# Moving the first normalisation statistics of a long-convolution and expert-mixture kernel beside its scalar setup, and loading its first column set in quarters

## The chip, the cores and the metric

The kernel runs on the 8 cores of one Trainium2 chip. Each core has TensorE (matmuls; PE in the profile), VectorE (DVE), ScalarE (ACT), GpSimd (POOL) and SyncE (SP, which issues DMAs), and 16 DMA engines. The eight cores run the same program on 2,048 of the 16,384 rows each and exchange nothing. The metric is the device time of the slowest core in microseconds.

## The reference

The input `x` has shape (2, 8192, 4096). Two residual layers are applied:

```python
x = x + s4(layernorm(x))
x = x + experts(layernorm(x))

def s4(u):                       # u: rows of length L = 4096
    K = kernel of length L, from Lambda, p, q, Vc, Ct, Bp and log_step
    y = irfft(rfft(u, 2L) * rfft(K, 2L))[..., :L]      # causal convolution
    return y + D[0] * u

def experts(x):                  # 64 experts, 16 of them for each row
    scores = x @ Wr.T            # top 16, softmax: gates G
    h = einsum('nd,krd->nkr', x, A)                    # rank 16
    return einsum('nkr,kdr->nd', h * G[:, :, None], B) * 2
```

The convolution kernel `K` is that of a 64-dimensional complex state-space model. It doesn't depend on `x`, and every core computes what it needs of it.

## The kernel before

All five engines have instruction lists that are written out by hand in program order. Each engine works through its own list in order, and waits on named counters (semaphores) are put between the instructions. `P.wait(eng, name, value)` puts a wait on an engine's list, `P.op(eng, fn, inc=name)` an instruction that raises a counter when it is done, `P.dma` a DMA, which raises its counter by 16 when it has landed and, unless told otherwise, is issued only when all earlier ones of the same counter have landed.

The 2,048 rows of a core are held transposed: 4,096 features in 32 blocks of 128 partitions, and four sets (`s` = 0 to 3) of 512 columns (rows of `x`). A set of float32 is 8 MB. The buffers `U0` and `U1` hold sets in turn.

*Start.* SyncE issues 21 small loads (constants and the state-space parameters, counter `ld0`). GpSimd issues 32 loads of the router weights `wrt_b` with a cast (counter `ldg`). Then all five engines wait for both counters, and SyncE issues set 0 as one DMA of 8 MB (L371, counter `uld`).

*Statistics, `emit_prep1`.* For each of the 32 blocks of a set: ScalarE casts the block to bfloat16 into one of four buffers (L259), TensorE adds it up over the partitions with a matmul into `ps1` (L264), GpSimd squares it (L272), and TensorE adds the squares up into `ps2` (L277). The steps are made in eight groups of four blocks. `emit_chain1` follows with ten instructions, each of which waits for the one before: five on VectorE (L289 to L293), Ln and Exp on ScalarE (L294, L295), one on VectorE (L296), a matmul on TensorE that spreads the result over the partitions (L297), and a copy to `Rb` on ScalarE (L298). For set 0 all of this stands at the start of the program (L372 to L377). For sets 1 to 3 the steps are put between the chunks of the set before.

*Setup of the state-space model, L379 to L565.* Its instructions go through the helper `so`. It makes each wait for all earlier ones, whatever the engine:

```python
def so(eng, fn):
    P.wait(eng, "seq")
    P.wait(eng, "sqd")
    P.wait(eng, "sqg")
    P.op(eng, fn, inc="seq")
```

The first of them is a memset on VectorE (L379), the second an Exp on ScalarE (L382), the next 41 are on VectorE (L383 to the negation ahead of L436), and then come small float32 matmuls in turn with VectorE copies. The setup leaves the convolution's matrices `cm_T`, `cm_ET`, `cm_O1T` and `cm_MtT` (the last one written at L565). Scratch tiles of the setup lie in the memory of `U1`, so SyncE loads set 1 only when the setup is done.

*Correction row.* A short serial chain (L568 to L616) pushes a column of ones through the same convolution, with TensorE (L583 to L604) and ScalarE (`c1stage`, L595, and the state, L607) in turn, and writes `c1row`.

*Main work of the first layer.* For each set, in eight chunks of four blocks: casts (L656), matmuls for the state and the outputs (L676, L699, L705), a product with `Rb` (L715) and the sum with `x` (L720). Each quarter of a set that is done is spilled to DRAM as float32 and bfloat16 (L727, L731). Sets 1 to 3 are loaded in four quarters of 2 MB (L629), one after another. The experts' weights `At_sb` are loaded from GpSimd's queue while set 3 is worked on.

*Second layer.* The spilled sets are read back (`X2`), normalised, scored, multiplied by the experts' first matrices (L965), gated, and multiplied by the second ones (L1053), with the residual sum on VectorE (L1060).

Of the kernel before, what the change touches and what calls it, by code (L numbers as in the profile page):

```python
# [78 lines left out]
def build_nc():  # L79
    nc = bass.Bass("TRN2", target_bir_lowering=False)  # L80

    u_in = nc.dram_tensor("u_in", [NS1, 128, NBLK * F1], F32, kind="ExternalInput")
# [122 lines left out]
    P = Plan(nc)  # L205
# [10 lines left out]
    rb_cnt = {}  # L216
# [7 lines left out]
    UB = [U0, U1]  # L224
# [4 lines left out]
    rb_cnt = {}  # L229
    tcv_after = []  # L230

    def chain(eng, fn):
        P.wait(eng, "sx")
        P.op(eng, fn, inc="sx")

    def uld_full(s):
        return 16 if s == 0 else 16 + 64 * s

    def uld_q(s, b):
        return 16 if s == 0 else 16 + 64 * (s - 1) + 16 * (b // 8 + 1)  # L240

    def emit_prep1(s):
        buf = UB[s % 2]
# [6 lines left out]
        for g8 in range(8):  # L250
            def step(g8=g8):
                for b in range(4 * g8, 4 * g8 + 4):
                    q = b % 2
                    w = b % 4
                    P.wait("scalar", "uld", uld_q(s, b))
                    if b >= 4:
                        P.wait("scalar", "t_s1", base_s1 + (b - 4) + 1)
                        P.wait("scalar", "g_sq", base_gq + (b - 4) + 1)
                    P.op("scalar", lambda e, b=b, w=w: e.copy(  # L259
                        UBF.ap()[:, w * 512:(w + 1) * 512], blk_ap(buf, b)), inc="s_ub")  # L260
                    P.wait("tensor", "s_ub", base_ub + b + 1)
                    if b == 0:
                        P.wait("tensor", "sx", sx_prev)
                    P.op("tensor", lambda e, b=b, w=w: e.matmul(  # L264
                        ps1.ap()[:, :], sumw.ap()[:, :],
                        UBF.ap()[:, w * 512:(w + 1) * 512],
                        start=(b == 0), stop=(b == NBLK - 1),
                        skip_group_check=True), inc="t_s1")
                    P.wait("gpsimd", "s_ub", base_ub + b + 1)
                    if b >= 2:  # L270
                        P.wait("gpsimd", "t_sq", base_sq + (b - 1))
                    P.op("gpsimd", lambda e, b=b, q=q, w=w: e.tensor_mul(  # L272
                        sqs.ap()[:, q * 512:(q + 1) * 512],
                        UBF.ap()[:, w * 512:(w + 1) * 512],
                        UBF.ap()[:, w * 512:(w + 1) * 512]), inc="g_sq")
                    P.wait("tensor", "g_sq", base_gq + b + 1)
                    P.op("tensor", lambda e, b=b, q=q: e.matmul(  # L277
                        ps2.ap()[:, :], sumw.ap()[:, :],
                        sqs.ap()[:, q * 512:(q + 1) * 512],
                        start=(b == 0), stop=(b == NBLK - 1),  # L280
                        skip_group_check=True), inc="t_sq")
# [3 lines left out]
    def emit_chain1(s, base_s1, base_sq):  # L285
        sl = s % 2
        P.wait("vector", "t_s1", base_s1 + NBLK)
        P.wait("vector", "t_sq", base_sq + NBLK)
        chain("vector", lambda e: e.tensor_scalar(M_AP, ps1.ap()[0:1, :], 1.0 / DM, None, ALU.mult))  # L289
        chain("vector", lambda e: e.tensor_scalar(V_AP, ps2.ap()[0:1, :], 1.0 / DM, None, ALU.mult))  # L290
        chain("vector", lambda e: e.tensor_mul(R_AP, M_AP, M_AP))
        chain("vector", lambda e: e.tensor_sub(V_AP, V_AP, R_AP))
        chain("vector", lambda e: e.tensor_scalar(V_AP, V_AP, EPS, None, ALU.add))  # L293
        chain("scalar", lambda e: e.activation(R_AP, V_AP, AF.Ln))  # L294
        chain("scalar", lambda e: e.activation(R_AP, R_AP, AF.Exp, scale=-0.5))  # L295
        chain("vector", lambda e, sl=sl: e.tensor_scalar(negmr.ap()[0:1, sl * 512:(sl + 1) * 512], M_AP, -1.0, None, ALU.mult))  # L296
        chain("tensor", lambda e: e.matmul(psX.ap()[:, :], onesrf.ap()[:, :], R_AP, start=True, stop=True))  # L297
        chain("scalar", lambda e, sl=sl: e.copy(Rb.ap()[:, sl * 512:(sl + 1) * 512], psX.ap()[:, :]))  # L298
        rb_cnt[s] = P.count("sx")


    def bload(fn):
        P.dma("sync", fn, "ld0", serialize=False)
# [10 lines left out]
    def gd(fn):  # L314
# [2 lines left out]
        P.wait("gpsimd", "sqg")  # L317
        P.dma("gpsimd", fn, "sqg")

    def so(eng, fn):  # L320
        P.wait(eng, "seq")
        P.wait(eng, "sqd")
        P.wait(eng, "sqg")
        P.op(eng, fn, inc="seq")

    bload(lambda e: e.dma_start(out=identf.ap(), in_=identf_in.ap()))
    bload(lambda e: e.dma_start(out=identb.ap(), in_=identb_in.ap()))
# [9 lines left out]
    def vs(name):  # L337
        if name not in VR:
            VR[name] = len(VR)
            assert len(VR) <= 36  # L340
        i = VR[name]
        return vrow.ap()[0:1, i * 64:(i + 1) * 64]
# [19 lines left out]
    for db in range(NBLK):  # L362
        gload(lambda e, db=db: e.dma_start(out=wrt_b.ap()[:, 66 * db:66 * (db + 1)],
                                           in_=wrt_in.ap()[128 * db:128 * (db + 1), :]))

    ONES64 = vs("o64")
    for eng in ("vector", "scalar", "tensor", "sync", "gpsimd"):
        P.wait(eng, "ld0", P.count("ld0"))
        P.wait(eng, "ldg", P.count("ldg"))

    P.dma("sync", lambda e: e.dma_start(out=UB[0].ap()[:, :], in_=u_in.ap()[0]), "uld")  # L371
    _steps0, _b1, _b2 = emit_prep1(0)  # L372
    for _st in _steps0:
        _st()
    emit_chain1(0, _b1, _b2)

    P.wait("tensor", "sx", rb_cnt[0])  # L377

    so("vector", lambda e: e.memset(ONES64, 1.0))  # L379
    ONE1 = onesrf.ap()[0:1, 0:1]  # L380

# [181 lines left out]
        w, k = w * 2, k + 1  # L563
    so("vector", lambda e: e.tensor_copy(cm_O1T.ap()[:, :], Vch.ap()[:, 0:512]))
    so("vector", lambda e: e.tensor_copy(cm_MtT.ap()[:, :], Tch[9].ap()[:, :]))  # L565

    ONEC = state.ap()[:, 1020:1021]
    so("vector", lambda e: e.memset(ONEC, 1.0))  # L568
# [51 lines left out]
    for s in range(1, NS1):  # L620
# [4 lines left out]
        for q in range(4):  # L625
            if s >= 2:
# [3 lines left out]
                out=buf.ap()[:, q * 4096:(q + 1) * 4096],  # L630
                in_=bass.AP(u_in, s * 128 * 16384 + q * 4096, [[16384, 128], [1, 4096]])), "uld")
# [3 lines left out]
    for s in range(NS1):  # L635
        buf = UB[s % 2]
        for eng in ("tensor", "vector", "scalar"):
            P.wait(eng, "uld", uld_full(s))
            if s == 0:
                P.wait(eng, "seq", PH0_DONE)  # L640
                P.wait(eng, "sqd", PH0_DMAD)
                P.wait(eng, "sqg", PH0_DMAG)
# [4 lines left out]
        def emit_ln1(ls, c):  # L647
            lbuf = UB[ls % 2]
            G = ls * NCH + c
            for j in range(4):  # L650
                b = 4 * c + j
                wslot = (c % 2) * 4 + j
                P.wait("scalar", "uld", uld_q(ls, b))
                if G >= 2:
                    P.wait("scalar", "t_cv", tcv_after[G - 2])
                P.op("scalar", lambda e, b=b, w=wslot, lbuf=lbuf: e.copy(  # L656
                    LN1.ap()[:, w * 512:(w + 1) * 512],
                    blk_ap(lbuf, b)), inc="v_ln")
# [6 lines left out]
        for c in range(NCH):  # L665
# [19 lines left out]
            for tb in range(NSUB):  # L685
# [23 lines left out]
                b = 4 * c + tb  # L709
# [14 lines left out]
            if c % 2 == 1:  # L724
                q = c // 2
                P.wait("scalar", "v_xe", vxe_b + 8 * (q + 1))
                P.dma("scalar", lambda e, s=s, buf=buf, q=q: e.dma_start(  # L727
                    out=bass.AP(xsp_f, s * 128 * 16384 + q * 4096, [[16384, 128], [1, 4096]]),
                    in_=buf.ap()[:, q * 4096:(q + 1) * 4096]), "spf")
                P.wait("gpsimd", "v_xe", vxe_b + 8 * (q + 1))  # L730
                P.dma("gpsimd", lambda e, s=s, buf=buf, q=q: e.dma_start(  # L731
                    out=bass.AP(xsp_b, s * 128 * 16384 + q * 4096, [[16384, 128], [1, 4096]]),
                    in_=buf.ap()[:, q * 4096:(q + 1) * 4096]), "spb")
# [13 lines left out]
            if s == 3 and c == 0:  # L747
                P.wait("gpsimd", "spf", 64 * 3)
                P.wait("gpsimd", "spb", 64 * 3)
                for db in range(16):  # L750
                    P.dma("gpsimd", lambda e, db=db: e.dma_start(
                        out=At_sb.ap()[:, db * 1024:(db + 1) * 1024],
                        in_=at_in.ap()[128 * db:128 * (db + 1), :]), "at1", serialize=False)
                for db in range(16, 32):
                    P.dma("gpsimd", lambda e, db=db: e.dma_start(
                        out=At_sb.ap()[:, db * 1024:(db + 1) * 1024],
                        in_=at_in.ap()[128 * db:128 * (db + 1), :]), "at2", serialize=False)

    P.wait("gpsimd", "t_h", 24)
    for kb in range(4):  # L760
        P.dma("gpsimd", lambda e, kb=kb: e.dma_start(  # L761
            out=Bt_lo.ap()[:, kb * DM:(kb + 1) * DM],
            in_=bt_in.ap()[128 * kb:128 * (kb + 1), :]), "btl", serialize=False)

    for s in range(NS1):
        P.wait("sync", "spb", 64 * (s + 1))
        if s == 0:
# [3 lines left out]
                out=X2[0].ap()[:, 0:8192],  # L771
                in_=bass.AP(xsp_b, 0, [[NBLK * F1, 128], [1, 8192]])), "x2h")
# [4 lines left out]
                out=X2[0].ap()[:, 8192:16384],  # L777
                in_=bass.AP(xsp_b, 8192, [[NBLK * F1, 128], [1, 8192]])), "x2l")
# [113 lines left out]
    def emit_gating_post(s):  # L892
        sl = s % 2
        for t in range(4):
# [5 lines left out]
                ghx.ap()[64:128, sl * 512 + 128 * t:sl * 512 + 128 * (t + 1)],  # L900
                psA.ap()[:, 1792 + 128 * q:1920 + 128 * q][0:64, :]))

    P.wait("tensor", "sx")
    for db in range(NBLK):
        P.op("tensor", lambda e, db=db: e.matmul(
# [111 lines left out]
    for kb in range(4, 8):  # L1017
        P.dma("gpsimd", lambda e, kb=kb: e.dma_start(
            out=Bt_hi.ap()[:, (kb - 4) * DM:(kb - 3) * DM],
            in_=bt_in.ap()[128 * kb:128 * (kb + 1), :]), "bhi")  # L1020
    for s2 in range(NS3):
# [7 lines left out]
        for q in range(4):  # L1029
# [3 lines left out]
                out=XF[s2 % 2].ap()[:, q * 2048:(q + 1) * 2048], in_=qsrc), "xfl")  # L1033
# [44 lines left out]
def _get_nc():  # L1078
    global _NC_CACHE
    if _NC_CACHE is None:  # L1080
        _NC_CACHE = build_nc()
    return _NC_CACHE
# [52 lines left out]
```

How the kernel before makes its waits and increments, by code:

```python
    def wait(self, eng, name, val=None):  # L42
        self.sem(name)
        v = self.counts[name] if val is None else val
        if v <= 0:
            return
        h = self.sems[name]
        self.ops[eng].append(lambda e, h=h, v=v: e.wait_ge(h, v))
# [1 line left out]
    def op(self, eng, fn, inc=None, amt=1):  # L50
        if inc is not None:
            h = self.sem(inc)
            self.counts[inc] += amt
            self.ops[eng].append(lambda e, fn=fn, h=h, a=amt: fn(e).then_inc(h, a))
        else:
            self.ops[eng].append(lambda e, fn=fn: fn(e))
```

## Time and profile before

| | |
|---|---|
| median of 3 runs | 1517.33 us (1516.63 to 1521.82) |
| profiled execution, its time | 1524.42 us |
| its span, slowest core (core 5) | 1522.8 us |
| spans of the eight cores | 1499.9 to 1522.8 us |
| TensorE busy | 1003.6 us, 66% |
| VectorE busy | 455.0 us, 30% |
| ScalarE busy | 195.4 us, 13% |
| GpSimd busy | 178.7 us, 12% |
| DMA, mean over the span | 123 GB/s |

The profile is of one execution on the slowest core. The span runs from its first to its last instruction, and the execution's own time is 1.6 us longer. Times in the views are microseconds from the start of the span. Where the profile gives a granted clock, 1.00 is TensorE's full speed of 2.4 GHz and 0.50 is 1.2 GHz. Lines such as L259 are lines of the kernel before; L48 is the helper that makes a wait, and L388 and L391 are helpers of the setup for VectorE instructions of two tiles and of a tile and a number.

### The profile page before, as it was taken

The numbers are of one execution on the slowest core, as the hardware profiler recorded it, in microseconds if no ns is written. First come the engines' busy times: TensorE is split into PE (matmuls) and PEld (weight loads), VectorE is DVE, ScalarE is ACT, GpSimd is POOL, SyncE is SP. The second block draws the span as 40 slices with busy tenths as digits, with TensorE's granted clock in tenths as the row PEclk, the third lists the DMA queues.
The fourth block names the chain that finished last, engine by engine and source line by source line (L and its number), as shares of the span: only waits on it lengthen the run. The fifth ranks groups of instructions, "written<-read, shape, count | busy, mean of one in ns | idle before, by whom it ended". The sixth has DMA issues, their size and how long they took to land.

```text
span 1522.8 us, 13264 instructions; the slowest of 8 cores (1499.9 to 1522.8 us)
## 1 busy us (share of the span) xinstructions
PE 1003.6 (66%) x3837; PEld 398.5 (26%) x3837; DVE 455.0 (30%) x954; ACT 195.4 (13%) x402; POOL 178.7 (12%) x221
## 2 busy tenths in 40 slices
PE   0425534677678569725368768858876917998895
PEld 0113313122222112202123322323332403443342
DVE  0032211536536347600522132131212002433342
ACT  0410002242342332100000010010001000000000
POOL 4620000161260342100000000000000000000000
PEclk9965555788888788866678778978878958999997
DMA  8200011873954625997300020020006074777785
GB/s 165 80 1 0 0 7 43 281 257 128 283 197 122 182 83 149 198 191 199 118 1 0 0 111 1 0 97 14 1 0 111 0 193 138 278 267 255 237 288 221
DMA packets 25088, 186.59 MB, mean 123 GB/s; under 512 B 7544, under 2 KB 8313, under 8 KB 12474
## 3 DMA queue, kind: packets, MB, share of 16 engines
q1 hardware_dynamic: 8842, 84.52, 16.0%
q0 software_dynamic: 12720, 34.11, 13.1%
q10 hardware_dynamic: 3456, 67.11, 12.3%
q8 instruction: 34, 0.56, 0.2%
q14 instruction: 36, 0.29, 0.1%
HBM read 119.15 MB, written 83.89 MB: 133 GB/s over the span
## 4 chain that ended last, share of the span: by engine, by line
PE 37%; DMA 26%; DVE 11%; issue 10%; POOL 6%; another core or an unknown queue 5%; ACT 3%; DVEq 1%; ACTq 0%; POOLq 0%; SPq 0%
PE psA L965 15%; DMA XF<-xsp_f 12%; DMA xsp_b<-U 6%; POOL sqs L272 4%; DMA Bt_hi<-bt_in 3%; PE psA L1053 3%; PE ps L811 3%; DMA U<-u_in 2%; PE psX L858 2%; DVE sqs L805 2%; PE psA L699 2%; DVE cvt L715 1%; PE ps L277 1%; PE psS L676 1%
## 5 line engine op out<-in xcount | busy, mean ns | idle before, releaser
L965 PE MATMUL psA<-X,At_sb 128*128 128x512 bf16 x1024 | 256.6, 414 | 0.0
L1053 PE MATMUL psA<-htl_b,Bt_hi 128*128 128x512 bf16 x512 | 136.7, 390 | 40.7 <-DMA Bt_hi<-bt_in 40.7
L1060 DVE SCALAR_TENSOR_TENSOR XF<-psA,XF 128x512 f32<-128x512 f32 x128 | 88.1, 691 | 198.2 <-PE psA L1053 116.3
L1053 PE MATMUL psA<-htl_a,Bt_lo 128*128 128x512 bf16 x512 | 136.6, 391 | 14.2 <-DVE XF L1060 14.2
L965 PEld LDWEIGHTS psA<-X,At_sb 128*128 128x128 bf16 x1024 | 106.8, 106 | 141.9 <-issue 43.9
L272 POOL TENSOR_TENSOR sqs<-ubf 128x512 bf16<-128x512 bf16 x128 | 130.9, 1054 | 65.6 <-ACT ubf L259 35.1
L264 PE MATMUL ps<-ubf,sumw 128*128 128x512 bf16 x128 | 58.6, 458 | 93.2 <-ACT ubf L259 93.2
L699 PE MATMUL psA<-ln1w,cm_T 128*128 128x512 bf16 x320 | 97.4, 405 | 0.0
L720 DVE TENSOR_TENSOR U<-U,cvt 128x512 f32<-128x512 f32 x128 | 89.8, 702 | 13.4
L259 ACT CAST ubf<-U 128x512 bf16<-128x512 f32 x128 | 74.2, 617 | 137.0 <-PE ps L264 42.7
L715 DVE TENSOR_TENSOR cvt<-psA,Rb 128x512 f32<-128x512 f32 x128 | 87.6, 685 | 12.0 <-PE psA L705 12.0
L277 PE MATMUL ps<-sqs,sumw 128*128 128x512 bf16 x128 | 56.2, 439 | 46.7 <-POOL sqs L272 46.5
L811 PE MATMUL ps<-sqs,sumw 128*128 128x512 bf16 x128 | 56.8, 479 | 39.4 <-DVE sqs L805 37.8
L656 ACT CAST ln1w<-U 128x512 bf16<-128x512 f32 x128 | 69.2, 615 | 92.7 <-DVE U L720 61.0
L1053 PEld LDWEIGHTS psA<-htl_b,Bt_hi 128*128 128x128 bf16 x512 | 51.3, 100 | 106.3 <-issue 49.2
L1053 PEld LDWEIGHTS psA<-htl_a,Bt_lo 128*128 128x128 bf16 x512 | 50.7, 100 | 78.5 <-issue 21.8
L805 DVE TENSOR_TENSOR sqs<-X 128x512 bf16<-128x512 bf16 x128 | 50.8, 423 | 44.6 <-PE ps L811 36.3
L684 DVE CAST state<-psS 128x512 bf16<-128x512 f32 x32 | 22.0, 687 | 135.2 <-PE psS L681 128.3
L989 DVE TENSOR_TENSOR htl_a<-psA,grep 128x512 bf16<-128x512 f32 x16 | 11.1, 691 | 168.7 <-ACT grep L985 168.7
L989 DVE TENSOR_TENSOR htl_b<-psA,grep 128x512 bf16<-128x512 f32 x16 | 11.0, 690 | 142.8 <-ACT grep L985 142.8
L761 POOL DMA_DIRECT2D Bt_lo<-bt_in x4 | 2.1, 545 | 426.4 <-PE psA L969 426.4
L705 PE MATMUL psA<-negmr,c1row 1*128 1x512 bf16 x128 | 51.8, 405 | 0.0
(228 smaller groups left out, 696.3 us busy)
## 6 DMA issues: line engine op xcount, KB each, us to landing
xsp_f<-U ACTq DMA_DIRECT2D x16, 2048.0 KB, 12.7
XF<-xsp_f SPq DMA_DIRECT2D x32, 1024.0 KB, 5.3
y_out<-XF ACTq DMA_DIRECT2D x8, 4096.0 KB, 17.7
U<-u_in SPq DMA_DIRECT2D x12, 2048.0 KB, 10.4
xsp_b<-U POOLq DMA_DIRECT2D x16, 1024.0 KB, 13.0
X<-xsp_b SPq DMA_DIRECT2D x3, 4096.0 KB, 13.8
At_sb<-at_in POOLq DMA_DIRECT2D x32, 256.0 KB, 52.5
X<-xsp_b SPq DMA_DIRECT2D x2, 2048.0 KB, 12.1
```

What stands on the lines that cost most here:

```text
L259: P.op("scalar", lambda e, b=b, w=w: e.copy(UBF.ap()[:, w * 512:(w + 1) * 512], blk_ap(buf, b)), inc="s_ub")
L272: P.op("gpsimd", lambda e, b=b, q=q, w=w: e.tensor_mul(sqs.ap()[:, q * 512:(q + 1) * 512], UBF.ap()[:, w * 512:(w + 1) * 512], UBF.ap()[:, ...
L277: P.op("tensor", lambda e, b=b, q=q: e.matmul(ps2.ap()[:, :], sumw.ap()[:, :], sqs.ap()[:, q * 512:(q + 1) * 512], start=(b == 0), stop=(b ...
L656: P.op("scalar", lambda e, b=b, w=wslot, lbuf=lbuf: e.copy(LN1.ap()[:, w * 512:(w + 1) * 512], blk_ap(lbuf, b)), inc="v_ln")
L699: P.op("tensor", lambda e, tb=tb, w=wslot, d=tb - jb, fst=fst, bank=bank: e.matmul(psA.ap()[:, bank * 512:(bank + 1) * 512], cm_T.ap()[:, ...
L715: P.op("vector", lambda e, bank=bank, sl=sl, q2=q2: e.tensor_mul(cvt.ap()[:, q2 * 512:(q2 + 1) * 512], psA.ap()[:, bank * 512:(bank + 1) * ...
L720: P.op("vector", lambda e, b=b, buf=buf, q2=q2: e.tensor_add(blk_ap(buf, b), blk_ap(buf, b), cvt.ap()[:, q2 * 512:(q2 + 1) * 512]), inc="v ...
L805: P.op("vector", lambda e, b=b, q=q, xb=xb: e.tensor_mul(sqs.ap()[:, q * 512:(q + 1) * 512], blk_ap(xb, b), blk_ap(xb, b)), inc="v_sq")
L811: P.op("tensor", lambda e, b=b, q=q: e.matmul(ps2.ap()[:, :], sumw.ap()[:, :], sqs.ap()[:, q * 512:(q + 1) * 512], start=(b == 0), stop=(b ...
L965: P.op("tensor", lambda e, kr=kr, db=db, pb=pb, xb=xb: e.matmul(psA.ap()[:, pb * 512:(pb + 1) * 512], At_sb.ap()[:, db * 1024 + kr * 128:d ...
L1053: P.op("tensor", lambda e, d=d, kbo=kbo, kb=kb, pb=pb, s1=s1, bt=bt: e.matmul(psA.ap()[:, pb * 512:(pb + 1) * 512], bt.ap()[:, kbo * DM + ...
L1060: P.op("vector", lambda e, dd=dd, pb=pb, xf=xf: e.scalar_tensor_tensor(xf.ap()[:, dd * 512:(dd + 1) * 512], psA.ap()[:, pb * 512:(pb + 1) ...
```

## The change

There are five edits.

1. Set 0 is loaded by four DMAs of 2 MB, one after another, in place of one of 8 MB. The functions that give the counter's values for a set and for a block follow.
2. VectorE, ScalarE and TensorE wait for `ld0` alone at the start. SyncE and GpSimd still wait for both counters. TensorE's wait for `ldg` now stands ahead of the first use of the router weights in the second layer.
3. The eight step groups of `emit_prep1(0)` are put in a list, `PRE0`. The helper `so` counts its instructions and, behind each fifth up to the 45th, takes a group off the list and emits it. Groups that are left would be emitted behind L565.
4. `emit_chain1(0, ...)` is emitted behind L565.
5. TensorE's wait for the `Rb` copy of set 0 ahead of the setup is gone. The main work's own wait for it stays.

```diff
     def uld_full(s):
-        return 16 if s == 0 else 16 + 64 * s
+        return 64 * (s + 1)
 
     def uld_q(s, b):
-        return 16 if s == 0 else 16 + 64 * (s - 1) + 16 * (b // 8 + 1)
+        return 64 * s + 16 * (b // 8 + 1)
...
+    PRE0 = []
+    SO_CTR = [0]
+
     def so(eng, fn):
         P.wait(eng, "seq")
         P.wait(eng, "sqd")
         P.wait(eng, "sqg")
         P.op(eng, fn, inc="seq")
+        SO_CTR[0] += 1
+        if SO_CTR[0] % 5 == 0 and SO_CTR[0] <= 45 and PRE0:
+            PRE0.pop(0)()
...
-    for eng in ("vector", "scalar", "tensor", "sync", "gpsimd"):
+    for eng in ("vector", "scalar", "tensor"):
+        P.wait(eng, "ld0", P.count("ld0"))
+    for eng in ("sync", "gpsimd"):
         P.wait(eng, "ld0", P.count("ld0"))
         P.wait(eng, "ldg", P.count("ldg"))
-
-    P.dma("sync", lambda e: e.dma_start(out=UB[0].ap()[:, :], in_=u_in.ap()[0]), "uld")
+    LDG_ALL = P.count("ldg")
+
+    for q in range(4):
+        P.dma("sync", lambda e, q=q: e.dma_start(
+            out=UB[0].ap()[:, q * 4096:(q + 1) * 4096],
+            in_=bass.AP(u_in, q * 4096, [[16384, 128], [1, 4096]])), "uld")
     _steps0, _b1, _b2 = emit_prep1(0)
-    for _st in _steps0:
-        _st()
-    emit_chain1(0, _b1, _b2)
-
-    P.wait("tensor", "sx", rb_cnt[0])
+    PRE0.extend(_steps0)
...
     so("vector", lambda e: e.tensor_copy(cm_MtT.ap()[:, :], Tch[9].ap()[:, :]))
+
+    while PRE0:
+        PRE0.pop(0)()
+    emit_chain1(0, _b1, _b2)
...
+    P.wait("tensor", "ldg", LDG_ALL)
     P.wait("tensor", "sx")
     for db in range(NBLK):
```

## Rows read from the trace of the kernel before

**Rows 1.** The cores, span and mean granted clock of each.

```profile
core 3: 1499.9 us, clock 0.811
...
core 5: 1522.8 us, clock 0.797
```

**Rows 2.** Stages: length; busy (count) PE, PEld, DVE, ACT, POOL; clock; DMA share; GB/s.

```profile
21.50:50.50 29.00, 0.00 (x0) 0.00 (x0) 0.00 (x0) 0.01 (x1) 0.00 (x0) 1.00 0.91 289
50.50:85.30 34.80, 21.11 (x64) 6.20 (x64) 0.00 (x0) 20.69 (x33) 31.97 (x32) 1.00 0.00 1
85.30:106.70 21.40, 2.04 (x2) 0.50 (x2) 11.87 (x48) 1.94 (x4) 0.00 (x0) 0.58 0.00 0
...
245.50:260.00 14.50, 6.49 (x148) 5.72 (x148) 0.34 (x2) 6.08 (x41) 0.56 (x1) 0.50 0.02 3
...
93.90:106.70 12.80, 8.25 (x41) 0.50 0.00 1
```

**Rows 3.** Timeline of the start, and SyncE's waits there (total, times, longest).

```profile
1.56 17.02 POOL L363 DMA_DIRECT2D wrt_b<-wrt_in  x32 [0.86 <-POOLq L80]
...
10.30 0.34 SPq L361 DMA_DIRECT2D vrow<-ls_in  x1
...
12.09 6.49 POOL L363 DMA_DIRECT2D wrt_b<-wrt_in  x12
...
SPq L48 <- DMA wrt_b<-wrt_in: 8.6, 1, 8.6
SPq L48 <- DMA vrow<-ls_in: 2.2, 1, 2.2
```

**Rows 4.** The chain that ended last: start, length, what.

```profile
21.56 28.87 DMA U<-u_in
```

**Rows 5.** Timeline of set 0's statistics, ScalarE and GpSimd.

```profile
50.49 1.28 ACT L259 ACT_TABLE_LOAD   x1 [50.49 <-DMA U<-u_in]
51.79 2.70 ACT L259 CAST ubf<-U 128x512 bf16<-128x512 f32 x5
...
52.56 6.02 POOL L272 TENSOR_TENSOR sqs<-ubf 128x512 bf16<-128x512 bf16 x6 [33.98 <-ACT ubf L259]
...
58.76 25.96 POOL L272 TENSOR_TENSOR sqs<-ubf 128x512 bf16<-128x512 bf16 x26 [0.19 <-ACT ubf L259]
```

**Rows 6.** Timeline of set 0's chain and of the setup's first instructions.

```profile
85.35 0.68 DVE L289 TENSOR_SCALAR svec<-ps 1x512 f32<-1x512 f32 x1 [85.35 <-PE ps L277]
...
89.00 0.63 ACT L294 ACTIVATE svec<-svec 1x512 f32<-1x512 f32 x1 [7.56 <-DVE svec L293]
...
93.15 0.59 ACT L298 COPY Rb<-psX 128x512 f32<-128x512 f32 x1 [2.80 <-PE psX L297]
93.63 0.20 ACT L382 ACTIVATE vrow<-vrow 1x1 f32<-1x1 f32 x1
93.93 0.15 DVE L383 RECIPROCAL vrow<-vrow 1x1 f32<-1x1 f32 x1 [2.99 <-ACT vrow L382]
...
106.74 0.44 PE L436 MATMUL psA<-vrow 1*64 1x64 f32 x2 [13.68 <-DVE vrow L391]
```

**Rows 7.** SyncE's loads of set 1, their landing, and L629 over the run.

```profile
259.75 0.33 SPq L629 DMA_DIRECT2D U<-u_in  x1
...
277.28 0.33 SPq L629 DMA_DIRECT2D U<-u_in  x1
...
U<-u_in SPq DMA_DIRECT2D x1, 2048.0 KB, 15.5
...
DMA to landing us min/median/max: 7.2/10.4/20.0
```

**Rows 8.** Timeline where the correction row's chain begins.

```profile
245.66 0.06 DVE L568 MEMSET state<- 128x1 bf16 x1 [0.21 <-DVE cm_MtT L565]
...
246.47 0.16 ACT L607 CAST state<-psS 128x1 bf16<-128x1 f32 x1
```

**Rows 9.** The chain that ended last, its longest piece in the middle.

```profile
616.32 73.06 another core or an unknown queue
```

## The prediction

> **What bounds the kernel now.** I began with the spans of the cores: 1499.9 to 1522.8 us [rows 1]. The change touches only what stands ahead of the four column sets' main work, so I took the table of stages next [rows 2]. The reader is to see that the first 260 us are a sequence of stages in which one engine or queue works while the others stand still. From 21.5 to 50.5 the DMA queues are busy (0.91) and no engine computes. From 50.5 to 85.3 three engines work on the first normalisation statistics and DMA is idle. From 85.3 to 106.7 VectorE is busy 11.87 us and TensorE 2.04 us. Such stages sit end to end on the path: what is laid over another comes off the span, if nothing new is waited for.
>
> The timelines of the start say when things can begin. SyncE issues its last small load at 10.30 and sees it land 2.2 us later, at 12.9; it then waits 8.6 us for the `wrt_b` loads, which GpSimd issues one after another in 17.02 us [rows 3]. At 21.56 it issues the whole 8 MB of set 0, which lands 28.87 us later [rows 4]. Then ScalarE loads its table, and GpSimd squares 32 blocks one after another, 52.56 to 84.72, 1.005 us each [rows 5]. So the order is: `wrt_b`, then set 0, then GpSimd, then the ten serial steps of `emit_chain1`, then 41 small VectorE instructions, and only at 106.74 the first matmul of the state-space setup [rows 6].
>
> **The change part by part.** *The vector instructions.* Counted in the code, instruction 44 through `so` is the first on TensorE. The eight statistics steps are emitted behind `so` numbers 5 to 40, that is all ahead of it on TensorE's queue, but they put nothing on VectorE. VectorE no longer waits for `wrt_b` either. Its work can thus start at 12.9. The Exp needs the table, 1.28 us, and 0.2 us for itself [rows 5, 6]; from the first reciprocal (93.93) to the matmul (106.74) is 12.81 us [rows 6]. It ends near 12.9 + 0.1 + 1.28 + 0.2 + 12.8 = 27.3. It is hidden behind the load of set 0; without that cover it would cost the 12.8 again, and there are over 35 us of cover left. The table load too goes under the wait, off the path.
>
> *The load in quarters.* Four DMAs of 2 MB, each issued when the last has landed. The nearest rows are the same kind of DMA for set 1, with no spill beside them: the first is issued at 259.75 and the third at 277.28, so a period of (277.28 - 259.75)/2 = 8.77 us [rows 7]. Four take 35.1 us, against 28.87 for the whole one: the last lands 6.2 us later than before, at 21.56 + 35.1 = 56.6. But GpSimd needs only 8.04 us for the eight blocks of a quarter, less than the period, so it has caught up when the last quarter lands. What remains is: 0.05 us to the cast, 0.77 to the first square (51.79 to 52.56), 8 x 1.005 = 8.04 for the squares, 0.63 to the point where the last matmul is done (84.72 to 85.35) [rows 5, 6]; together 9.5. TensorE is free at 56.6 + 9.5 = 66.1, where it was free at 85.3.
>
> Bounds of the period: 7.2 us is the shortest quarter anywhere. Then GpSimd is the bound, 21.56 + 7.2 + 0.82 + 32 x 1.005 + 0.63 = 62.4. The median is 10.4, over transfers that mostly ran beside spills [rows 7]: 21.56 + 41.6 + 9.5 = 72.7. I take 8.77, as its rows are the only ones without a spill.
>
> The Trainium skill (DMA: Bandwidth & Descriptors, Anatomy of one DMA) gives about 2.0 us fixed plus bytes over 436 GB/s for a DMA from GpSimd's queue; as an estimate from that page a quarter would take 6.8 us, GpSimd would be the bound and the sum would be about 4 us better than mine. The rows disagree: by that rule the whole load would take 21.2 us, and it took 28.87.
>
> *First matmul of the setup.* With the vector part long done it starts at 66.1 in place of 106.74: a gain of 40.6 us. The 64 statistics matmuls stand ahead of it on TensorE, so a late quarter now delays the setup directly.
>
> *emit_chain1 moved.* Its steps come behind the setup's last VectorE copy and ahead of the correction row's chain. Nothing can cover them there: VectorE's memset of ONEC and TensorE's c1 matmuls are queued behind them, and ScalarE's `c1stage` copies behind the `Rb` copy. From the first step to the end of the `Rb` copy is 93.15 + 0.59 - 85.35 = 8.39 us [rows 6]; four small copies of about 0.6 in all then lead to the first state copy, which stood 0.81 behind the memset's place (246.47 - 245.66) [rows 8]. So + (8.39 + 0.6 - 0.8) = + 8.2 us. TensorE's granted clock there is 0.50, its level of 1.2 GHz, after the setup's small matmuls; in the old place it had fallen too, with a mean of 0.58 over that stage [rows 2]. I take no difference.
>
> *The other edits.* The wait on `ldg` at the weight sums comes hundreds of microseconds after those loads landed: 0. The changed counts in `uld_full` and `uld_q` only follow the quarters: 0. SyncE still waits for `wrt_b`, so set 0 is not issued earlier.
>
> *Sum:* -40.6 + 8.2 = -32.4 us. Everything behind is started by what comes before it, not at a fixed time: even the longest wait of the middle, 73.06 us, follows loads that GpSimd issues when a set is stored [rows 9]. So I carry the sum to the end. The profiled execution: 1524.42 - 32.4 = 1492. It stands 7.1 us above the median of the runs; for that, 1517.3 - 32.4 = 1485.
>
> **The rivals.** *Slow quarters.* The third quarter of set 1 took 15.5 us and the slowest one of any set 20.0, beside spills [rows 7]. At 12 us the last lands at 69.6, TensorE is free at 79.1 and the sum is -27.6 + 8.2 = -19.4, so 1498. *Slower than before:* the same mechanism, from a period T on at which 21.56 + 4T + 9.5 + 8.2 exceeds 106.74, that is T = 16.9; at 20 us the sum is +12.6, so 1530. Against it: there is no spill from 21 to 56, and the whole load made 7.2 us per 2 MB with all eight cores loading.
>
> *The vector instructions hold up GpSimd.* They now run from 12.9 on, while GpSimd still issues the last eleven or so of the 32 `wrt_b` loads (twelve from 12.09 on), on which SyncE waits before set 0 [rows 3]. VectorE is busy 8.25 us in its 12.8 us [rows 2] (the last of these rows is of VectorE alone); if none of GpSimd's issuing could go on beside it, set 0 would be up to 8.3 us late and the sum -24, so 1493. Nothing in the trace speaks for it, as no VectorE work lies beside those issues there. The Trainium skill (SBUF — State Buffer, SBUF: two separate sides) says that some VectorE instructions lock GpSimd out while it writes descriptors; no row here shows it.
>
> *Table loads return.* The table that was loaded ahead of a cast at 50.49 [rows 5] still serves the Ln at 89.00, which begins as soon as its input is there [rows 6]. With Exp now first, another table might be chosen and changed once at the moved Ln: +1.3 us, 1486. This is inside the range.
>
> *The clock or the memory takes the gain back.* Core 3 ended at 1499.9 with clock 0.811, core 5 at 1522.8 with 0.797 [rows 1]: 1.6 us for each 0.001. To lose the whole 32 us the mean clock would have to fall by 0.020, more than the cores differ. For it: the whole run is denser by a fixed idle piece. A part of that, 5 to 10 us either way, is the noise of my forecast. *No gain* would need some such effect of 25 us, so 1517.
>
> **How the numbers follow.** Forecast 0.76 (own range 1475 to 1496); slow quarters 0.07; vector work holding up GpSimd 0.05; GpSimd-bound prep by quarters of 7.2 us, with -44.3 + 8.2 = -36.1, so 1481, 0.05; no gain 0.04; slower 0.03. I put the range at 1473 to 1502: from the bound of 36 us and 8 us of spread between cores to the case of 12 us quarters and 4 us more. One measurement tells this kernel from no change at about 0.5%, or 7.6 us. Faster by more 0.93, within it 0.04, slower 0.03.
>
> **What the profile after would show.** The vector instructions of the setup between 13 and 28 us; a table load near 13; four loads of set 0 that land near 30, 39, 48 and 57; squares in four groups with small gaps; the first setup matmul at 66; the ten chain steps right behind the cast of `cm_MtT` near 205, and set 1 issued near 227 in place of 259.75. The prediction is wrong if the quarters take over 12 us, if `wrt_b` is issued later than before, or if set 1 starts 32 us earlier and the end does not.

## The result and the profile after

The changed kernel took 1483.39 us (median of 8 runs, 1478.95 to 1485.25), the kernel before in the same comparison 1520.33 us (8 runs, 1516.63 to 1526.77). The ratio is 0.9752, 95% interval 0.9733 to 0.9772: 37.7 us less, 34.7 to 40.6. The prediction was a change of 32.4 us and a time of 1485 us, with a range of 1473 to 1502. Some executions of any of these kernels show a lower granted clock on one die or both and take some per cent longer; the ratios below leave them out, the medians beside them don't.

The profiled execution took 1482.69 us; the span of its slowest core (core 7) is 1481.0 us. This is the timeline of its start, SyncE, VectorE, ScalarE and GpSimd; it answers to [rows 3] and the first part of [rows 6].

```profile
1.56 17.02 POOL L369 DMA_DIRECT2D wrt_b<-wrt_in  x32 [0.86 <-POOLq L80]
...
13.28 0.11 DVE L387 MEMSET vrow<- 1x64 f32 x1 [13.28 <-DMA vrow<-ls_in]
13.47 1.28 ACT L390 ACT_TABLE_LOAD   x1 [13.47 <-DVE vrow L387]
14.76 0.20 ACT L390 ACTIVATE vrow<-vrow 1x1 f32<-1x1 f32 x1
15.07 0.15 DVE L391 RECIPROCAL vrow<-vrow 1x1 f32<-1x1 f32 x1 [1.68 <-ACT vrow L390]
...
21.34 28.11 SPq L381 DMA_DIRECT2D U<-u_in  x4
...
27.26 0.43 DVE L399 TENSOR_SCALAR vrow<-vrow 1x1 f32<-1x1 f32 x2
```

The vector instructions of the setup now lie between 13.28 and 27.69, 12.62 us from the reciprocal to the end of the last; in the old place it was 12.66 (93.93 to 106.59). GpSimd's issue of `wrt_b` takes 17.02 us, to the hundredth what it took without VectorE beside it.

GpSimd's squares of set 0, and the first matmul of the setup (L444, which was L436), answer to [rows 5] and the end of [rows 6]:

```profile
31.48 8.07 POOL L272 TENSOR_TENSOR sqs<-ubf 128x512 bf16<-128x512 bf16 x8 [12.89 <-ACT ubf L259]
...
41.29 8.02 POOL L272 TENSOR_TENSOR sqs<-ubf 128x512 bf16<-128x512 bf16 x8 [1.75 <-ACT ubf L259]
...
50.07 8.02 POOL L272 TENSOR_TENSOR sqs<-ubf 128x512 bf16<-128x512 bf16 x8 [0.76 <-ACT ubf L259]
...
58.42 8.02 POOL L272 TENSOR_TENSOR sqs<-ubf 128x512 bf16<-128x512 bf16 x8 [0.34 <-ACT ubf L259]
...
66.89 0.32 PE L444 MATMUL psA<-vrow 1*64 1x64 f32 x2
```

The reader is to see four groups of eight with gaps of 1.75, 0.76 and 0.34 us in which GpSimd waits for a cast of the next quarter: on this core the DMAs set the pace, and not by much. On core 0 the same row reads x32 without a gap, and there GpSimd is the bound; its first setup matmul comes at 62.9. The eight cores split evenly: in each pair of neighbours (0 and 1, 2 and 3, and so on) one core's quarters took 7.9 to 8.0 us from issue to landing (median of its four), the other's 8.6 to 9.0. In a second execution it was 7.8 to 7.9 and 8.6 to 9.3. No run shows why.

The moved chain, behind the cast of `cm_MtT` (L573), and the issue of set 1; they answer to [rows 6, 8] and the first of [rows 7]:

```profile
201.81 0.23 DVE L573 CAST cm_MtT<-Tch 128x128 bf16<-128x128 f32 x1 [0.17 <-DVE cm_O1T L572]
201.99 0.68 DVE L289 TENSOR_SCALAR svec<-ps 1x512 f32<-1x512 f32 x1
...
207.65 2.04 PE L297 MATMUL psX<-svec,onesrf 1*128 1x512 f32 x2 [7.20 <-DVE negmr L296]
...
209.78 0.59 ACT L298 COPY Rb<-psX 128x512 f32<-128x512 f32 x1 [2.80 <-PE psX L297]
...
210.47 0.22 ACT L619 CAST state<-psS 128x1 bf16<-128x1 f32 x1
...
223.85 0.33 SPq L641 DMA_DIRECT2D U<-u_in  x1
```

From the cast of `cm_MtT` to the first state copy it is 210.47 - 201.81 = 8.66 us. Before it was 246.47 less the cast's start, which lay 0.43 ahead of the memset of [rows 8]: 1.24 us. The chain thus costs 7.4 us here.

The eight cores differ by some microseconds, so I read three marks on every core of every execution, and put their means over the eight cores side by side in this document: the start of the first setup matmul, the start of the cast of `cm_MtT`, and the first issue of set 1. The last column is the start of the last matmul of the second layer.

| mean over the cores, us | first setup matmul | cast of cm_MtT | set 1 issued | last matmul |
|---|---|---|---|---|
| before, the execution of the prediction | 105.8 | 242.9 | 257.4 | 1496.7 |
| before, a second execution (`c_before`) | 105.3 | 242.1 | 256.6 | 1492.2 |
| changed | 64.5 | 200.5 | 222.5 | 1460.7 |
| changed, a second execution (`c_after`) | 64.5 | 200.2 | 222.2 | 1457.8 |

From the issue of set 1 to that last matmul the four executions need 1239.3, 1235.6, 1238.2 and 1235.5 us. So the gain is made ahead of set 1 (34.9 us between the first executions, 34.4 between the second) and carried to the end; two executions of one kernel differ by 2.6 and 3.8 us behind that mark.

### The profile page after: what moved, and what is told of

It reads as the page before. It is cut to its first block, busy times and chain, and to the rows that moved or that the text cites. A ratio compares the mean times of both kernels' runs of the same rounds, so it can differ in the third digit from the quotient of the medians.

```text
span 1481.0 us, 13267 instructions; the slowest of 8 cores (1467.8 to 1481.0 us)
## 1 busy us (share of the span) xinstructions
PE 995.0 (67%) x3837; PEld 395.6 (27%) x3837; DVE 454.5 (31%) x954; ACT 193.8 (13%) x402; POOL 178.8 (12%) x221
## 4 chain that ended last, share of the span: by engine, by line
PE 37%; DMA 27%; DVE 11%; issue 9%; POOL 6%; another core or an unknown queue 5%; ACT 4%; DVEq 1%; ACTq 0%; POOLq 0%; SPq 0%
PE psA L978 15%; DMA XF<-xsp_f 13%; DMA xsp_b<-U 6%; POOL sqs L272 3%; DMA Bt_hi<-bt_in 3%; PE psA L1066 3%; PE ps L823 3%; PE psA L711 2%; DMA U<-u_in 2%; DVE sqs L817 2%; PE psX L870 2%; DVE cvt L727 1%; PE psS L688 1%; PE ps L277 1%
## 5 line engine op out<-in xcount | busy, mean ns | idle before, releaser
L978 PE MATMUL psA<-X,At_sb 128*128 128x512 bf16 x1024 | 252.9, 410 | 0.0
L277 PE MATMUL ps<-sqs,sumw 128*128 128x512 bf16 x128 | 56.9, 445 | 44.4 <-POOL sqs L272 44.2
```

What stands on the lines that cost most here:

```text
L277: P.op("tensor", lambda e, b=b, q=q: e.matmul(ps2.ap()[:, :], sumw.ap()[:, :], sqs.ap()[:, q * 512:(q + 1) * 512], start=(b == 0), stop=(b ...
L978: P.op("tensor", lambda e, kr=kr, db=db, pb=pb, xb=xb: e.matmul(psA.ap()[:, pb * 512:(pb + 1) * 512], At_sb.ap()[:, db * 1024 + kr * 128:d ...
```

## The experiments

### One part at a time

`e1_quarters` is the kernel before with the quarters alone:

```diff
-    P.dma("sync", lambda e: e.dma_start(out=UB[0].ap()[:, :], in_=u_in.ap()[0]), "uld")
+    for q in range(4):
+        P.dma("sync", ..., "uld")        # and uld_full, uld_q as in the change
```

> The kernel before with the load of set 0 in quarters, and nothing moved. Theory of the prediction (the terms add up): the last quarter lands near 57, TensorE is free near 66 in place of 85.3, the chain and the vector instructions stay behind it as before, so the first matmul of the setup (L436 before) comes at 87 to 88 in place of 106.7: 19 us less than before, about 1501. The table load is hidden in the slack of the first quarter and counts in this. Rival, the gain is the quarters' alone and the vector instructions cost nothing on the path: the whole 37 us, about 1483. Rival, the quarters give nothing since four waits eat it: within 5 us of before.

`e2_move` is the changed kernel with set 0 loaded whole (and the counter's values for it as before):

```diff
-    for q in range(4):
-        P.dma("sync", ..., "uld")
+    P.dma("sync", lambda e: e.dma_start(out=UB[0].ap()[:, :], in_=u_in.ap()[0]), "uld")
```

> The changed kernel with set 0 loaded whole again: only the moves. Theory: set 0 lands near 50.3, the squares end near 83.4, the first matmul of the setup comes near 84.0 in place of 106.7 (22.7 us less), and the chain at its new place gives 7.4 us back as in the changed kernel: 15 us less than before, about 1505. Rival, the moves carry the whole gain: about 1483. Rival, the moved chain costs as much as the vector instructions save: about 1520.

Quarters alone: 1491.51 us, ratio 0.9841 (0.9811 to 0.9871), 24 us less. Moves alone: 1493.37 us, ratio 0.985 (0.9825 to 0.9874), 23 us less. The marks:

| mean over the cores, us | first setup matmul | set 1 issued | against before | expected |
|---|---|---|---|---|
| `e1_quarters` | 85.8 | 236.6 | -20.8 | -19 |
| `e2_move` | 82.2 | 240.2 | -17.2 | -15 |

GpSimd's row in `e2_move` (core 3) shows the whole set worked off without a gap from 49.60 on, straight after the landing and with no table load ahead of it:

```profile
49.60 6.02 POOL L272 TENSOR_TENSOR sqs<-ubf 128x512 bf16<-128x512 bf16 x6 [31.01 <-ACT ubf L259]
55.84 25.95 POOL L272 TENSOR_TENSOR sqs<-ubf 128x512 bf16<-128x512 bf16 x26 [0.23 <-issue]
```

Both rivals that gave the whole gain to one part fall. Neither part reaches the change's set 1 at 222.5 alone. The two add up to 38.0 against 34.9 for both. The table load's 1.28 us should come off the path by either (by the quarters only where the DMAs set the pace), and so count twice in the sum; that is argued, and the other 1.8 us are open. The measured times lie 3 and 6 us below what the marks give, as those of the other variants do by 0.5 to 5 us. A second execution of before, `c_before`, was taken to see whether the surplus lies ahead of set 1:

> The kernel before once more, one look, on the chip of the runs beside it. In all variants so far the end came 2 to 6 us earlier than the earlier issue of set 1 explains, measured against the one profiled execution of before. Theory: that is the spread of single executions, and here set 1 is issued within 1 us of 257.4 in the mean of the cores, and the last matmul group begins between 1490 and 1500. Rival: an execution of before on the same chip has set 1 at 260 or later, and the surplus lies ahead of it.

Set 1 was issued at 256.6, and the last matmul began at 1492.2, 4.5 us earlier than in the first execution of before. Of that, 0.8 us lies ahead of the mark and 3.8 behind it: the first execution was a long one, so a part of the surplus is the spread of executions. It need not be all: behind set 1 the nine variants of this document take 1230.0 to 1234.5 us, and before and changed 1235.5 to 1239.3. So in these executions the surplus lies behind set 1; why all variants are shorter there isn't shown.

### The quarters in flight together

`e5_in_flight` gives each quarter of set 0 a counter of its own, so that SyncE issues all four at once:

```diff
     for q in range(4):
         P.dma("sync", lambda e, q=q: e.dma_start(
             out=UB[0].ap()[:, q * 4096:(q + 1) * 4096],
-            in_=bass.AP(u_in, q * 4096, [[16384, 128], [1, 4096]])), "uld")
+            in_=bass.AP(u_in, q * 4096, [[16384, 128], [1, 4096]])), f"uq{q}")
```

> The changed kernel with the four quarters of set 0 on counters of their own, all issued at once. Theory, the four waits for the landing cost some 6 us against the whole load, and quarters of one queue are served in their order: the first lands near 30 as before, the last near 50, GpSimd is then the bound and TensorE is free near 63.5 in place of 66.9, 3 us less than the changed kernel, about 1480. Rival, the four are served side by side, the first lands near 50 too, and the squares begin only then: TensorE is free near 84, 17 us more, about 1500.

1476.59 us, ratio 0.9738 (0.9711 to 0.9766). GpSimd's squares on core 3, and the stages of that core (length, busy time and count of PE, PEld, DVE, ACT, POOL, then clock, DMA share, GB/s):

```profile
31.15 6.02 POOL L272 TENSOR_TENSOR sqs<-ubf 128x512 bf16<-128x512 bf16 x6 [12.57 <-ACT ubf L259]
37.39 25.95 POOL L272 TENSOR_TENSOR sqs<-ubf 128x512 bf16<-128x512 bf16 x26 [0.23 <-issue]
...
36.00:41.00 5.00, 3.60 (x11) 0.99 (x10) 0.00 (x0) 2.86 (x6) 4.78 (x6) 1.00 0.99 321
41.00:46.00 5.00, 2.98 (x11) 0.96 (x10) 0.00 (x0) 3.10 (x6) 5.00 (x6) 1.00 0.99 323
46.00:51.00 5.00, 2.98 (x11) 0.96 (x10) 0.00 (x0) 3.10 (x6) 5.00 (x6) 1.00 0.55 195
```

The quarters are served in their order: the squares begin at 31.15 and not near 50, and the DMA engines are busy 0.99 until they are done near 49. From issue to landing the quarters take 9.4 us (shortest), 19.2 (median) and 27.9 (longest) on this core. The waits between the quarters do cost landing time: on core 7 the last quarter landed just ahead of its cast at 57.60 in the changed kernel, and by 49.9 here. On core 3, one of those with the faster loads, it is about 2 us (issued at 44.3 and landed 7.4 us later at the earliest, against 50.1 here). But the first setup matmul moved only from 64.5 to 63.6 in the mean of the cores, and set 1 from 222.5 to 221.5. What the DMAs won, GpSimd as the next bound kept. The expected 3 us were for a core like 7, where the matmul came at 63.3 in place of 66.9; the mean core had less to win. The difference between the two times is within their intervals.

### The chain: at its old place, and in the setup's DMA waits

`e3b_chain_early` is the changed kernel with the chain behind the last statistics group, ahead of the first setup matmul:

```diff
             PRE0.pop(0)()
+            if not PRE0 and len(PB) == 2:
+                emit_chain1(0, *PB)
+                PB.append(0)
+                P.wait("tensor", "sx", rb_cnt[0])
...
-    emit_chain1(0, _b1, _b2)             # behind the cast of cm_MtT
```

> The changed kernel with the ten chain instructions at their old place, behind the last statistics group and ahead of the setup's first matmul, TensorE waiting for them. Theory: nothing covers them there either, so the first setup matmul comes 8 us later (72.5 in the mean of the cores) and the end of the stretch 7 us earlier: set 1 within 2 us of the changed kernel's 222.2, the time within 3 us of it. Rival: at the end they are dearer, and the old place wins 5 us or more.

1481.28 us, ratio 0.9779 (0.974 to 0.9817). The first setup matmul came at 73.7 in the mean of the cores, 9.2 us later, and set 1 at 224.8, 2.3 and 2.6 us later than in the two executions of the changed kernel. By this mark, of one execution, the end is the better place, by a little more than the 2 us that I allowed; the times don't tell the two apart (0.9729 to 0.9791 for the changed kernel, below). A small part of it is TensorE: in the changed kernel L444 (two matmuls) took 0.32 us straight behind the statistics, and here, behind the chain, the same pair took 0.44 (core 3):

```profile
72.39 2.04 PE L297 MATMUL psX<-svec,onesrf 1*128 1x512 f32 x2 [5.77 <-DVE negmr L296]
75.36 0.44 PE L451 MATMUL psA<-vrow 1*64 1x64 f32 x2 [0.93 <-ACT Rb L298]
```

`e4_chain_gaps` puts the ten instructions where every engine waits for a small DMA of the setup:

```diff
     sd(lambda e: e.dma_start(out=kp_dram.ap(), in_=kp_sb.ap()))
+    chain_some(2)
...
     for d in range(4):
         sd(lambda e, s=src: e.dma_start(out=Xt[2].ap()[:, :], in_=s))
+        chain_some((3, 3, 1, 1)[d])
...
-    emit_chain1(0, _b1, _b2)             # behind the cast of cm_MtT
```

> The changed kernel with the ten instructions of the moved chain put into the setup's DMA waits: two behind the store of kp_dram, then three, three, one and one behind its four loads. Theory: the chain's 7.4 us at the end are uncovered work, and each of the waits (some 3 us in which no engine works) covers its part, so 6 to 7 us less than the changed kernel, about 1477. Rival, the pieces lengthen the waits, since the VectorE copies that end each wait are queued behind them: 0 to 3 us less, 1480 to 1483. Rival, the end of this stretch is not on the path that sets the end: no difference, 1483.

1468.17 us, ratio 0.969 (0.966 to 0.972). Timeline of the waits, core 6:

```profile
157.91 0.67 DVE L300 TENSOR_SCALAR svec<-ps 1x512 f32<-1x512 f32 x1
158.05 0.24 SPq L555 DMA_DIRECT2D kp_dram<-kp_sb  x1
158.68 0.68 DVE L301 TENSOR_SCALAR svec<-ps 1x512 f32<-1x512 f32 x1
159.38 0.55 PE L562 MATMUL psX<-vrow,onesrf 1*128 1x1 f32 x2 [3.48 <-DMA kp_dram<-kp_sb]
...
160.44 13.20 SPq L566 DMA_DIRECT2D Xt<-kp_dram  x4
160.99 0.68 DVE L303 TENSOR_TENSOR svec<-svec 1x512 f32<-1x512 f32 x1
...
163.31 0.76 PE L570 MATMUL psA<-Xt,jrev 128*128 128x128 f32 x2 [3.38 <-DMA Xt<-kp_dram]
```

TensorE still waits for the DMAs (3.48, 3.38 us) and not for VectorE, so the rival of longer waits falls. From the store of `kp_dram` to the cast of `cm_MtT` it is 44.0 us in the mean of the cores, 44.4 in the changed kernel; from the cast to set 1 14.6 in place of 22.0. Set 1 is issued at 215.1, 7.4 us earlier than in the changed kernel: the chain's whole price. The place, and not the instructions, was what it cost.

### What bounds the start now

`e6_no_wrt_wait` lets SyncE issue set 0 without waiting for `wrt_b`:

```diff
-    for eng in ("sync", "gpsimd"):
-        P.wait(eng, "ld0", P.count("ld0"))
-        P.wait(eng, "ldg", P.count("ldg"))
+    P.wait("sync", "ld0", P.count("ld0"))
+    P.wait("gpsimd", "ld0", P.count("ld0"))
+    P.wait("gpsimd", "ldg", P.count("ldg"))
```

> The changed kernel with SyncE waiting for the small loads alone, so that set 0 is issued near 13 in place of 21.4; GpSimd keeps its wait for wrt_b. Theory: the chain wrt_b, set 0, squares, setup bounds the start, so 8.4 us earlier at its head are worth 5 to 8 us at the first matmul of the setup (57 to 60 in place of 64.5 in the mean of the cores), less what the wrt_b loads take of the DMA queues. Rival: set 0's packets hold up the wrt_b loads, on whose landing GpSimd's squares wait, and the squares start no earlier than near 30: 0 to 2 us.

The changed kernel again, beside it:

> The changed kernel once more, unaltered, as the mark for the three beside it on this chip. By the two earlier results its ratio to the kernel before is 0.975. The prediction's sum of 32.4 us gives 0.979; the traces so far show set 1 issued 34.9 us earlier in the mean of the cores, which gives 0.977.

The changed kernel took 1476.73 us (ratio 0.976, 0.9729 to 0.9791), without the wait 1470.8 us (0.9717, 0.9683 to 0.975). The first setup matmul came at 58.3 in place of 64.5, set 1 at 215.7 in place of 222.2: 6.5 us. On core 0 GpSimd's squares begin at 24.29, and not near 30 as the rival had it; the last thing that they waited for is `wrt_b`:

```profile
24.29 6.02 POOL L272 TENSOR_TENSOR sqs<-ubf 128x512 bf16<-128x512 bf16 x6 [5.71 <-DMA wrt_b<-wrt_in]
```

`e7_spread` takes the statistics matmuls off the path: each of the 64 goes behind one of the setup's matmuls, from the fifth on, and casts and squares are emitted together at the start.

```diff
     def so(eng, fn):
...
         SO_CTR[0] += 1
-        if SO_CTR[0] % 5 == 0 and SO_CTR[0] <= 45 and PRE0:
-            PRE0.pop(0)()
+        if SO_CTR[0] == 5:
+            emit_prep0()                 # all casts and squares; TensorE's 64 pieces into PEQ
+        if eng == "tensor":
+            TO_CTR[0] += 1
+            if TO_CTR[0] >= 5 and PEQ:
+                PEQ.pop(0)()
```

> The changed kernel with the 64 statistics matmuls of set 0 put one by one behind the setup's matmuls from the fifth on, in place of all ahead of the first; casts and squares are emitted together at the start. Theory: what is left of the first 66 us on the path is the statistics that stand ahead of the setup on TensorE's queue; without them the setup starts near 28 in place of 64.5, and each piece of some 0.45 us runs while VectorE copies, so that the setup gets longer by 5 to 25 us of the 37 won: 12 to 32 us less than the changed kernel, 1452 to 1472. Rival: every piece adds its whole 0.6 us to the serial setup, 38 us in all, and nothing is won: 1483. Rival: the pieces wait for GpSimd's squares of 1.0 us each: the setup stands still as before, 1483 or more.

1445.01 us, ratio 0.9551 (0.9516 to 0.9586), 31.7 us less than the changed kernel beside it, by the medians and by the ratios. The setup's first matmul comes at 27.1, 37.4 us earlier, and the setup is 5.0 us longer (140.7 us to the cast of `cm_MtT`, in place of 135.7); set 1 is issued at 189.8, 32.4 us earlier. Core 0 over this stretch (columns as in the stage rows above), first of the changed kernel in its second execution, `c_after`:

```profile
64.40:200.20 135.80, 61.30 (x178) 40.24 (x177) 31.97 (x120) 0.00 (x0) 0.00 (x0) 0.51 0.01 2
```

and with the statistics spread:

```profile
26.40:168.30 141.90, 87.69 (x241) 43.33 (x241) 34.91 (x120) 19.39 (x32) 33.15 (x32) 1.00 0.15 53
```

TensorE, ScalarE and GpSimd do the statistics in time that the setup had left idle. VectorE's same 120 instructions take 2.94 us more, about half of the 6.1 us that this core's setup grew by; why is told in the last section. The other half wasn't separated.

`e8_spread_gaps` adds the chain in the DMA waits, and `e9_all` the issue of set 0 without the wait for `wrt_b`; their diffs are those of `e4_chain_gaps` and `e6_no_wrt_wait`.

> As the run before, and the ten chain instructions in the setup's DMA waits, as in the run that tried these alone (there set 1 was issued 7.4 us earlier in the mean of the cores). Theory: the two are independent and add up, 7 us less than the run before. Rival: the last pieces of the statistics come so late that the chain no longer finds the waits empty: less than 4 us.

> The spread statistics and the chain in the DMA waits, as before, and set 0 issued without the wait for wrt_b. Theory: with the statistics beside the setup neither set 0 nor GpSimd is on the path, so the edit that gave 6 us to the changed kernel gives nothing here: set 1 within 2 us of 182.7, ratio to the kernel before 0.950 as without it. Rival: the first statistics pieces wait for their data (TensorE stands at the pieces before 36), and earlier data save 2 to 5 us.

| | time, us | ratio to before | first setup matmul | set 1 issued |
|---|---|---|---|---|
| `e7_spread` | 1445.01 | 0.9551 | 27.1 | 189.8 |
| `e8_spread_gaps` | 1440.12 | 0.9502 (0.9466 to 0.9538) | 26.9 | 182.7 |
| `e9_all` | 1437.97 | 0.9489 (0.9464 to 0.9514) | 28.4 | 183.0 |

The chain's 7.1 us at set 1 come on top in full. The earlier set 0, worth 6.5 us in the changed kernel, is worth nothing at set 1 here: its load and the squares are no longer on the path. (The first setup matmul even comes 1.5 us later, for a reason given in the last section, and the setup behind it is 1.2 us shorter.) The last two can't be told apart by their times. Either beats both kernels: `e8_spread_gaps` is 5.0% under the kernel before.

## Why the prediction was right, point by point

| term | predicted, us | measured, us |
|---|---|---|
| first setup matmul | 66.1, from 106.74 on core 5: -40.6 | 65.6 on core 5; mean 64.5 from 105.8: -41.3 |
| setup itself | 0 | 136.0 in place of 137.1: -1.1 |
| chain at its new place | +8.2 | 22.0 in place of 14.5 from the cast to set 1: +7.5 |
| set 1 | -32.4 | -34.9 |
| end | -32.4 | -37.7 by the ratio (-34.7 to -40.6) |

*The vector instructions* were hidden whole, between 13.28 and 27.69, where 12.9 to 27.3 had been worked out. The table load went with them, at 13.47.

*The load in quarters.* The period was 8.77 us in the sum. On core 7, by the casts at 30.71 and 57.60, it was 8.96 ((57.60 - 30.71)/3); on core 0 GpSimd never waited, the case that had been the lower bound, 62.4, and TensorE got to the setup at 62.9. So both mechanisms of the sum, DMA pace and GpSimd pace, occurred at once on different cores. The four cores with the slower loads (1, 2, 5 and 7) reached the setup at 66.2 in the mean, where 66.1 was forecast; the other four at 62.8. The prediction took one pace for all cores and gave the other a chance of 0.05. The estimate of 6.8 us for a quarter, from the Trainium skill (DMA: Bandwidth & Descriptors, Anatomy of one DMA), is not borne out: of the 32 quarters on the eight cores the shortest took 7.2 us from issue to landing and the longest 10.1.

*The setup* was put down as unchanged. It is 1.1 us shorter. A part of that is that its first matmuls run straight behind the statistics, 0.32 us for a pair that took 0.44 [rows 6].

*The chain* was priced at 8.2 us and cost 7.5. The ten steps took the 8.4 us that they had taken before; two small terms beside them were too large. The first step waits for none of the setup's counters and started 0.18 us behind the start of the cast (201.81 to 201.99), where the sum had put it in the memset's place, 0.43 behind. And the first state copy began 0.10 us behind the end of the `Rb` copy (210.37 to 210.47), where 0.6 us had been put down for the small copies.

*Slow quarters* did not occur: none took 12 us. *Vector work holding up GpSimd* did not either: the 32 issues took 17.02 us with VectorE beside the last eleven. *Table loads* did not return: Ln and Exp in the moved chain start as soon as their inputs are there, as before. *The clock* did not take the gain back: its mean over the eight cores was 0.8045 before and 0.8055 after, in the profiled executions. *No gain* and *slower* fell with the result.

The mechanism is the one forecast, term by term. The range of 1473 to 1502 held the time. Of the 5.3 us between the forecast change and the measured one, 2.5 us lie ahead of set 1, by the terms above, all three in the same direction. The other 2.8 us have no term, and the traces do not place them: at the last matmul the two pairs of executions are 36.0 and 34.4 us apart. The measured interval begins at 34.7 us, so they are not clear of noise. That the time itself, 1483.39 us, came within 2 us of 1485 is partly luck: the kernel before stood at 1520.33 us in the comparison, 3 us above the 1517.3 that the forecast had started from, and this made up for most of the larger gain. The forecast for the profiled execution, 1492, was off by 9 us: it carried over 7.1 us by which the first execution of before had stood above the median, and these belonged to that one execution.

## What to carry to other kernels

When a start is a row of stages with one engine at work in each, add up what each stage would cost with the others laid over it, engine by engine, and ask where the in-order queues still force an order. Here the 64 statistics matmuls ahead of the setup on TensorE's queue were what kept 37 us on the path after the change, and giving each of them a slot behind a setup matmul won 32 of these. The serial chain was free in the stretch where everything waited for a DMA, and cost its whole length where nothing did; its two uncovered places differed by 2 to 3 us.

## What the runs showed of the hardware

*GpSimd held VectorE up.* In `e7_spread` VectorE works on SBUF tiles beside GpSimd's squares. First the squares and then VectorE, core 2:

```profile
30.95 3.03 POOL L258 TENSOR_TENSOR sqs<-ubf 128x512 bf16<-128x512 bf16 x3 [12.38 <-ACT ubf L253]
...
32.20 0.84 DVE L503 TENSOR_SCALAR smat<-smat,dcol 64x64 f32<-64x64 f32 x1
33.14 0.89 DVE L504 TENSOR_SCALAR smat<-smat,dcol 64x64 f32<-64x64 f32 x1
34.13 0.22 DVE L440 TENSOR_TENSOR smat<-smat 64x64 f32<-64x64 f32 x1
34.46 0.24 DVE L506 TENSOR_SCALAR smat<-smat,dcol 64x64 f32<-64x64 f32 x1
```

The three squares end near 31.96, 32.97 and 33.98. L503 ends at 33.04 and L504 at 34.03, each just behind a square, and each takes 0.6 us longer than L506, the same form with no square beside it. VectorE's copies out of PSUM took 0.292 us with and without squares beside them. On core 0 a few instructions on SBUF tiles hold nearly all of the 2.94 us: these two 1.24 us, four 64x64 `tensor_tensor` on `smat` 0.84 us (0.426 us each in place of 0.217), and one 128x128 on `Sch` 0.82 us (1.110 in place of 0.291). `e9_all` shows it once more, core 5, at the end of the setup's vector instructions, where the first two squares run from 26.36 to 28.39:

```profile
26.65 1.75 DVE L451 TENSOR_TENSOR vrow<-vrow 1x1 f32<-1x1 f32 x2
```

In the changed kernel the same two took 0.40 us, with GpSimd idle. These 1.35 us are most of the 1.5 us by which the first setup matmul came later in `e9_all` than in `e8_spread_gaps`. I had looked for this the other way about, VectorE holding up GpSimd's DMA issues, which did not happen. The Trainium skill (SBUF — State Buffer, Who interferes with whom) has a rule for it: the two engines share a pair of SBUF ports, VectorE uses that pair for instructions with two SBUF inputs or in a two-port mode, and whichever starts first keeps it for its whole instruction. The rows of the `tensor_tensor` instructions agree. Whether L503 and L504, which have one tensor input, ran in a two-port mode is not shown.

*The granted clock and the matmuls' durations parted.* In the setup of `e7_spread` the granted clock was 1.00 and in the changed kernel's 0.51 (the two stage rows above; over the matmuls named next, 47.8 to 77.5 and 80.0 to 109.5 on core 0, it was 1.00 and 0.50, the levels of 2.4 and 1.2 GHz). The 24 matmuls of the setup from `Sch` and `Tch`, 128x128 float32, took 486 ns (median) in both. The mean clock of core 0 rose from 0.799 to 0.857 with it. A higher mean clock in the profile was thus no sign of faster matmuls in this stretch.
